# A row sum on TensorE moved from ahead of the mix to between the two linear halves of a tile

## The reference: what is computed

```
W = weights[condition]                       # (64, 64, 64)
y = einsum('bct,bcd->bdt', x, W)             # the mix
w = (unpacked.astype(float32) - zero_point) * scale    # (1024, 1024), 6-bit integers unpacked
out = x + einsum('bsk,nk->bsn', y, w) + bias # the linear layer
```

## Time and profile before

| | us |
|---|---|
| median of 3 runs | 309.73 |
| lowest and highest | 307.82, 311.16 |
| the profiled execution | 310.09 |
| its span in the profile | 307.9 |

### The profile page before, as it was taken

The page is one execution under the profiler, slowest core; times in us unless marked ns, Lnnn a source line. Parts: engine busy times, 40 slices in busy tenths (PEclk is TensorE's granted clock), DMA queues, the critical chain, the costliest instruction groups (busy, mean ns, idle before and its releaser), DMA issues.

```text
span 307.9 us, 8409 instructions
## 1 busy us (share of the span) xinstructions
PE 293.3 (95%) x3236; PEld 243.0 (79%) x3236; DVE 207.7 (67%) x261; ACT 79.1 (26%) x169; POOL 78.3 (25%) x39
## 2 busy tenths in 40 slices
PE   8695599999999999999999999999999999999995
PEld 3584478888888888888888888888888888888885
DVE  3569985666666777666666776666666776667554
ACT  3664125222112222222112222221122222210000
POOL 1008305432113333332123333321133333321000
PEclk9989599999999999999999999999999999999999
DMA  6992065544333333244343332343343311110221
GB/s 221 285 375 99 3 209 188 173 146 142 119 131 140 106 137 115 98 140 140 106 140 126 118 136 87 128 140 117 130 140 106 138 71 68 68 70 34 84 89 68
DMA packets 20689, 39.54 MB, mean 128 GB/s; under 512 B 6850, under 2 KB 7106, under 8 KB 20674
## 3 DMA queue, kind: packets, MB, share of 16 engines
q1 hardware_dynamic: 20674, 39.33, 36.8%
HBM read 22.54 MB, written 16.78 MB: 128 GB/s over the span
## 4 chain that ended last, share of the span: by engine, by line
PE 90%; DVE 5%; SPq 1%; DMA 1%; issue 1%; DVEq 0%
PE o_ps L286 77%; PE y_ps L249 11%; DMA q_raw<-in_L_ffn_qweight_dram 1%; PE ysum_ps L263 1%; DVE q_int L422 1%; DVE q_int L420 1%; DVE q_int L424 1%; DVE q_bf L429 1%; PE y_ps L286 1%; PE o_ps L271 1%; DVE y_lo L437 0%; SPq L145 0%; SPq L141 0%; SPq L136 0%; SPq L174 0%
## 5 line engine op out<-in xcount | busy, mean ns | idle before, releaser
L286 PE MATMUL o_ps<-qT,y_hi 128*128 128x512 f32 (+1 forms) x512 | 203.7, 399 | 0.0
L286 PE MATMUL o_ps<-qT,y_lo 128*128 128x512 f32 (+1 forms) x512 | 200.1, 392 | 0.0
L542 POOL TENSOR_TENSOR resid<-x_sb,bias_bc 128x1024 f32<-128x1024 f32 x32 | 77.2, 2415 | 198.9 <-DVE o_sb L465 176.8
L286 PEld LDWEIGHTS o_ps<-qT,y_hi 128*128 128x128 f32 x512 | 97.0, 190 | 21.6
L286 PEld LDWEIGHTS o_ps<-qT,y_lo 128*128 128x128 f32 x512 | 97.1, 190 | 19.7
L457 DVE TENSOR_TENSOR o_sb<-o_ps,scale_bc 128x512 f32<-128x512 f32 x63 | 43.5, 691 | 71.6 <-PE o_ps L286 69.7
L360 ACT ACTIVATE y_hi<-y_ps 128x512 fp32r<-128x512 f32 x64 | 34.8, 596 | 181.4 <-PE y_ps L249 181.4
L446 DVE SCALAR_TENSOR_TENSOR resid<-zs_bc,ysum,resid 128x1024 f32<-128x1024 f32 x32 | 60.0, 1874 | 0.0
L437 DVE TENSOR_TENSOR y_lo<-y_ps,y_hi 128x512 fp32r<-128x512 f32 x64 | 41.2, 686 | 13.6 <-ACT y_hi L360 13.6
L465 DVE TENSOR_TENSOR o_sb<-o_sb,resid 128x512 f32<-128x512 f32 x63 | 43.6, 692 | 2.7 <-DVE resid L446 0.5
L249 PE MATMUL y_ps<-w_sb,x_sb 64*64 64x64 f32 x2048 | 37.8, 223 | 0.3 <-DMA w_sb<-in_L_cond_weights_dram 0.3
(11 more groups left out here) (25 smaller groups left out, 39.7 us busy)
## 6 DMA issues: line engine op xcount, KB each, us to landing
x_sb<-in_x_dram SPq DMA_DIRECT2D x32, 512.0 KB, 3.3
out_dram<-o_sb SPq DMA_DIRECT2D x63, 256.0 KB, 2.0
q_raw<-in_L_ffn_qweight_dram SPq DMA_DIRECT2D x8, 384.0 KB, 5.4
w_sb<-in_L_cond_weights_dram SPq DMA_DIRECT2D x64, 16.0 KB, 1.9
scale_bc<-_L_ffn_weight_scale_dram SPq DMA_DIRECT2D x1, 512.0 KB, 6.7
zs_bc<-n_weight_zero_point_dram SPq DMA_DIRECT2D x1, 512.0 KB, 7.5
bias_bc<-in_L_ffn_bias_dram SPq DMA_DIRECT2D x1, 512.0 KB, 8.3
out_dram<-o_sb SPq DMA_DIRECT2D x2, 128.0 KB, 1.9
```

The costliest lines, as they stand in the source:

```text
L286: last = nc.tensor.matmul(bank, part[:, slot, kt, :], qT[:, kt, col:col + width], start=(kt == 0 and part is y_hi), stop=(kt == KT - 1 and ...
L542: nc.gpsimd.tensor_tensor(resid[:, j % RING, :], x_sb[:, j % RING, :], bias_bc[:], ALU.add).then_inc(xbias_ready, 1)
```

## The change

`sum_y` goes from ahead of the mix to between the two linear halves of a tile. `wait_mix` of the next mix goes ahead of the last two matmuls of half 1. On ACT `copy_ysum` and `sum_x` change places, and `sum_x`'s scratch output gets two buffers. The start-up's order of PE stays, but for one `wait_mix` ahead of the loop.

```diff
--- before.py
+++ after.py
@@ -76,7 +76,7 @@
         xsum = sb("xsum", [P, RING], F32)
         ysum = sb("ysum", [P, RING], F32)
         warm = sb("warm", [P, 512], BF16)
-        junk = sb("junk", [P, K], BF16)
+        junk = sb("junk", [P, 2, K], BF16)
         resid = sb("resid", [P, RING, N], F32)
         o_sb = sb("o_sb", [P, 2, N], F32)
 
@@ -280,22 +280,26 @@
                     pe.wait_ge(scaled[h], t)
                 products(o_ps[:, h, :], h * NH, NH, j % RING).then_inc(o_ps_ready[h], 1)
 
-            def products(bank, col, width, slot):
-                for kt in range(KT):
+            def products(bank, col, width, slot, kts=range(KT)):
+                for kt in kts:
                     for part in (y_hi, y_lo):
                         last = nc.tensor.matmul(bank, part[:, slot, kt, :], qT[:, kt, col:col + width],
                                                 start=(kt == 0 and part is y_hi),
                                                 stop=(kt == KT - 1 and part is y_lo))
                 return last
 
-            def step(j, i, mixes=True):
+            def step(j, i, mixes=True, ahead=True):
+
                 if mixes:
-                    wait_mix(j + LEAD, i)
+                    mix(j + LEAD, i)
+                linear(j, i, 0)
+                if mixes:
                     sum_y(j + LEAD, i)
-                    mix(j + LEAD, i)
-                for h in range(H):
-                    linear(j, i, h)
-
+                pe.wait_ge(scaled[1], i * RING + j)
+                products(o_ps[:, 1, :], NH, NH, j % RING, range(KT - 1))
+                if ahead:
+                    wait_mix(j + LEAD + 1, i)
+                products(o_ps[:, 1, :], NH, NH, j % RING, range(KT - 1, KT)).then_inc(o_ps_ready[1], 1)
 
             pe.wait_ge(warm_ready, 1)
             for _ in range(WARMUP):
@@ -331,11 +335,12 @@
                 sum_y(j + RING, 0)
             for h in range(H):
                 linear(3, 0, h)
+            wait_mix(LEAD, 1)
             with pe.Fori(1, TRIPS - 1) as i:
                 for j in range(RING):
                     step(j, i)
             for j in range(RING - 1):
-                step(j, TRIPS - 1, mixes=j + LEAD < RING)
+                step(j, TRIPS - 1, mixes=j + LEAD < RING, ahead=False)
             linear(RING - 1, TRIPS - 1, 0)
             pe.wait_ge(scaled[1], TILES - 1)
             for bank, col, width in last_pieces:
@@ -348,7 +353,7 @@
                 x_arrived(act, j, i)
                 if not isinstance(i, int) or i * RING + j >= RING:
                     act.wait_ge(ysum_ps_ready, i * RING + j - RING + 1)
-                nc.scalar.activation(junk[:], x_sb[:, j % RING, :], ACT.Copy,
+                nc.scalar.activation(junk[:, j % 2, :], x_sb[:, j % RING, :], ACT.Copy,
                                      accum_out=xsum[:, j % RING:j % RING + 1]).then_inc(xsum_ready, 1)
 
             def high(j, i):
@@ -396,9 +401,10 @@
             def step(j, i, highs=True, sums=True):
                 if highs:
                     high(j + LEAD, i)
-                    copy_ysum(j + LEAD, i)
                 if sums:
                     sum_x(j + LEAD + 1, i)
+                if highs:
+                    copy_ysum(j + LEAD, i)
 
             for j in range(1, RING):
                 step(j, 0)
```

## The result

The changed kernel takes 313.31 us (median of 4 runs, 312.80 to 313.71) against 309.44 us before: a ratio of 1.0108, with a 95% interval of 1.0066 to 1.0149 (the two medians alone would give 1.0125, inside it). The forecast was 312.5 us, slower by 0.9%. The profiled execution takes 312.80 us with a span of 310.8, against 310.09 and 307.9.

What follows compares the result with a forecast made beforehand. PE bounds the kernel, busy 293.3 of 307.9 us. Per tile +0.22 - 0.11 = +0.11 us, times 25 is +2.8 on the profiled 310.09, giving 312.9; less 0.36 for the median, 312.5 us, range 308.4 to 315.5.

Steps and rivals of the forecast that it cites:

- The seam ahead of the mix: From last linear matmul to mix in the loop: without the row sum 0.32 for 0.43, 0.11 us less per tile.
- The waits at nothing: Moving the mix's waits ahead of half 1's last two matmuls on PE costs nothing, as they were met long before.
- Rival A: Ahead of the mix, its loads start under the last linear matmul; seam 0.23, total 308.6 us; chance 0.14.
- The row sum's new place at 0.22: Between the linear halves, two uncovered full-width loads of 0.11 each cost 0.22 us per tile.
- rival B: One of the two loads between the halves is covered; row sum costs 0.11 there, total 309.7 us; chance 0.10.
- rival C: Loads between the halves don't overlap; row sum costs 0.40, tile 0.29 longer, total 317.0 us; chance 0.09.
- The sum: Per tile in the loop +0.22 - 0.11 = +0.11 us, times 25 tiles +2.8 us.
- What moved at no cost: SP's reload about 1.1 us later, ACT's row-sum copy some 5 us later, all hidden behind PE.
- Rival D: A wait holds PE up: reload held by the later row sum, or late x; open upwards; 0.05 with unknown.

Runs made afterwards that it cites:

- small row sum between the halves: Changed kernel with the row sum made of two 64x64 matmuls, between the halves, its waits ahead of half 0's last two matmuls: period 9.013 us.

## Why the prediction was right

**The seam ahead of the mix.** Forecast 0.11 less. Measured 0.43 to 0.32. The three parts of the seam hold: with one load fewer it is 0.32, with two more 0.66. The row sum's whole price there is 0.154 all the same, since it also slowed half 0 by 0.037, which the forecast didn't have.

**The waits at nothing.** Right, as far as it was tested: ratio 1.0001 with the waits early and the row sum in its old place. Rival A, loads that go ahead once the waits are gone, is refuted by the changed kernel itself: the mix's first load starts 0.32 after the last linear matmul with nothing between. Of the two rules of the Trainium skill that were weighed, that of TensorEngine Tiling (Key Properties), a drain at each change of the tiling mode, is the one that this case agrees with: at each change from full width to 64x64 in the loop, with or without waits and row sum ahead of it, the loads begin some 0.09 late, at the mix and at the small row sum between the halves alike. That of TensorE: Matmul & The Clock Gate (Part 2), loads pulled ahead of matmuls in flight, agrees here with the full-width loads of linear parts and row sum alone; the loop's 64x64 loads start 0.32 after the last matmul of 512 columns and not with it.

**The row sum's new place at 0.22.** The loads are right: two steps of 0.11 that nothing covers, where rival B needed one and rival C some 0.4. The sign that the prediction set for this was badly drawn: half 1 was to start 0.45 after the last matmul of half 0, or 0.34 by rival B. It starts at 0.37 (157.797 to 158.163), nearer to B, since a matmul starts 0.03 after its own load starts, so that a part of the second load shows in the step behind it. It is the load of y_lo that stands at 0.45, the second matmul of half 1 that comes 0.22 late (158.48 - 157.80 = 0.68 for two steps of 0.23), and the period that rules out B, which had 8.73. The whole price is 0.247, since the linear matmuls behind the break are slower for a while, 0.02 in all.

**The sum.** The forecast had +0.11 per tile, the period shows +0.093. What was missing in it is the slower linear matmuls behind a break: they cost 0.04 in half 0 before (3.574 against 3.537), which the change gives back, and 0.02 in half 1 now. So -0.115 - 0.037 + 0.247 = +0.095, the measured 0.093 within the rounding, and 25 tiles make 2.3 us where 2.8 was said. That the missing term took so little off the sum is luck, for it entered on both sides: each price alone was too low, by 0.04 and by 0.03. The median, 313.31, came out 0.8 above the forecast. What that is stays open; the start-up alone scatters by more (64.35 to 65.88). The better measured ratio, 1.0087, is 312.7 us on a kernel of 309.99, and its interval holds both 2.3 and 2.8 us.

**What moved at no cost.** The reload comes 1.15 us later (forecast 1.1), ACT's copy stands right behind the row sum, and PE has no hole. The copy comes 3.0 us later in the period than before (5.17 after the mix against 2.18), not the 5 of the prediction, which left out that the copy stood behind those of y's high part before. Rival D did not come about.

## What to carry to other kernels

In this kernel a tiny matmul cost TensorE the weight loads that no long matmul covered, and hardly its own columns: 0.01 us where one load fitted under the last matmul before a break that existed anyway, 0.16 where the same matmul broke a dense stream. So try small matmuls at a seam that is already paid, and in the tiling shape of their neighbour (0.067 behind the mix, 0.440 between the halves). The fp32 row sum had two loads, and its own matmul of one column covered the second in none of these traces. Before waits are moved, look whether the loads behind them already start under the matmul before: here they did, and moving the waits was worth nothing.

## What was not expected of the hardware

After every break in these traces (mix, row sum, change of shape) the next 5 to 10 linear matmuls start mostly 0.23 to 0.24 us apart and then settle at 0.227. It is 0.04 more behind the mix when one full-width fp32 row sum stands ahead of it (half 0 at 3.574 against 3.537), with the waits early or late, but not with two row sums there, where the seam grew by 0.22 and the period by only 0.180. Between the halves two row sums make it worse by 0.04. What sets it is not known; it moved the periods by up to 0.04 from what the loads say.

The same four small row-sum matmuls cost 0.100 ahead of the mix and 0.067 behind it. The trace shows that ahead they go in turn with the mix's first ones, two and two, in two groups; why that is dearer was not tried.
